# Finding the median magnitude of each token: a 31-step bisection replaced by a sum, six false-position counts and an eight-largest pass

## The reference

```python
xn = _layernorm(x)
# branch 1: a gated unit in which half of the gate's values are set to zero
s = silu(xn @ w_gate.T)                     # 2048 x 2752
idx = top_k(-abs(s), 1376)                  # the 1376 of smallest magnitude in each row
s[rows, idx] = 0
out1 = (s * (xn @ w_up.T)) @ w_down.T
# branch 2: relu(xn @ up_w)**2 @ down_w  +  (((xn @ fc1_w) @ expert_w) * route) @ fc2_w, then a layernorm
out = x + out1 + out2
```

## Time and profile before

| | us |
|---|---|
| runs: median of 3 (lowest, highest) | 2320.54 (2317.87, 2321.05) |
| the profiled execution, from its first to its last instruction | 2316.5 |
| PE busy in it | 2300.8 (99%) |
| DVE, ACT, POOL busy | 1674.1, 1112.2, 927.2 |
| DVE in the 248 counting passes of the bisection | 780.3 |
| ACT in its 248 | 655.9 |

### The profile page before, as it was taken

The page is one execution under the profiler, slowest core; times in us unless marked ns, Lnnn a source line. Parts: engine busy times, 40 slices in busy tenths (PEclk is TensorE's granted clock), DMA queues, the critical chain, the costliest instruction groups (busy, mean ns, idle before and its releaser), DMA issues.

```text
span 2316.5 us, 27959 instructions
## 1 busy us (share of the span) xinstructions
PE 2300.8 (99%) x10432; PEld 1912.1 (83%) x10432; DVE 1674.1 (72%) x1834; ACT 1112.2 (48%) x1307; POOL 927.2 (40%) x746
## 2 busy tenths in 40 slices
PE   8999999999999999999999999999999999999999
PEld 6888888888888888888888888888888888888887
DVE  4349999986366999998334599998723569999850
ACT  3247776223243688822124379780213457976110
POOL 5468988797354321333024423035004441302600
PEclk9999999999999999999999999999999999999999
DMA  7798988868899765575678875556567886555655
GB/s 285 276 402 315 334 320 305 266 238 310 300 361 331 244 227 191 195 248 178 235 232 277 283 253 193 197 193 242 203 221 254 282 268 239 192 192 195 232 191 179
DMA packets 202184, 583.61 MB, mean 252 GB/s; under 512 B 21568, under 2 KB 30784, under 8 KB 200512
## 3 DMA queue, kind: packets, MB, share of 16 engines
q1 hardware_dynamic: 202048, 581.82, 72.8%
HBM read 446.40 MB, written 135.33 MB: 251 GB/s over the span
## 4 chain that ended last, share of the span: by engine, by line
PE 82%; DVE 10%; DMA 3%; issue 2%; ACT 1%; SPq 1%; POOL 1%; DVEq 0%; ACTq 0%
PE bank L1065 26%; PE bank L1067 26%; PE bank L1066 26%; DVE junk_v L1414 3%; DVE prod L1481 2%; PE bank L1085 2%; DVE junk_v L1422 2%; DMA mixed_w<-mixes 1%; DMA split_w<-w 1%; DVE prod L1344 1%; PE bank L1076 1%; DVE acc L1385 0%; DMA w<-mixed_w 0%; SPq L631 0%; SPq L627 0%
## 5 line engine op out<-in xcount | busy, mean ns | idle before, releaser
L1414 DVE TENSOR_SCALAR_CACHE_REDUCE junk_v<-mag,cand 128x2816 bf16<-128x2816 f32 x248 | 780.3, 3146 | 8.8
L901 ACT ACTIVATE junk_s<-mag,cand 128x2816 uint8<-128x2816 f32 x248 | 655.9, 2645 | 191.6 <-DVE cand L1406 172.9
L1065 PE MATMUL bank<-w,tok 128*128 128x512 f32 (+1 forms) x808 | 309.9, 384 | 0.2 <-POOL w L845 0.2
L1067 PE MATMUL bank<-w,tok 128*128 128x512 f32 (+1 forms) x808 | 308.3, 381 | 0.0
L1066 PE MATMUL bank<-w,tok 128*128 128x512 f32 (+1 forms) x808 | 308.0, 381 | 0.0
L845 POOL TENSOR_TENSOR w<-raw,w 128x512 fp32r<-128x512 f32 (+1 forms) x196 | 267.9, 1370 | 76.5 <-ACT w L889 66.7
L1065 PE MATMUL bank<-w,prod_t 128*128 128x512 f32 x672 | 269.4, 401 | 0.0
L1067 PE MATMUL bank<-w,prod_t 128*128 128x512 f32 x672 | 262.8, 391 | 0.0
L1066 PE MATMUL bank<-w,prod_t 128*128 128x512 f32 x672 | 261.9, 390 | 0.0
L859 POOL TENSOR_TENSOR squares<-squares 128x512 f32<-128x512 f32 x64 | 67.4, 1054 | 463.9 <-ACT hidden L994 463.9
L1065 PE MATMUL bank<-tok,w 128*128 128x512 f32 x640 | 249.0, 389 | 0.0
(11 more groups left out here) (166 smaller groups left out, 4066.5 us busy)
## 6 DMA issues: line engine op xcount, KB each, us to landing
w<-split_w SPq DMA_DIRECT2D x498, 512.0 KB, 3.4
split_w<-w SPq DMA_DIRECT2D x188, 512.0 KB, 5.3
w_more<-split_w SPq DMA_DIRECT2D x66, 512.0 KB, 5.3
w<-mixed_w SPq DMA_DIRECT2D x126, 256.0 KB, 3.6
w_more<-mixed_w SPq DMA_DIRECT2D x66, 256.0 KB, 3.5
rows<-x_dram SPq DMA_DIRECT2D x32, 512.0 KB, 5.4
raw<-w_down_dram SPq DMA_DIRECT2D x44, 256.0 KB, 4.1
raw<-w_up_dram SPq DMA_DIRECT2D x40, 256.0 KB, 3.2
```

The source lines that it names most:

```text
L901: act.activation(junk_s[:, :, :], mag[:, :, t, :], ACT.Sign, scale=-1.0, bias=cand[:, t:t + 1], accum_out=cnt[:, t:t + 1]).then_inc(counte ...
L1065: pe.matmul(out, left[0], right[0], start=first, stop=False)
L1067: return pe.matmul(out, left[1], right[0], start=False, stop=last)
L1414: dve.tensor_scalar(junk_v[:, :, :], mag[:, :, t, :], cand[:, t:t + 1], float(1 - (GATED - KEPT)), ALU.is_lt, ALU.add, accum_out=cnt[:, t: ...
```

## The change

The bisection is taken out of the main path. In its place stand, for each block:

- `start_search`: three small memsets for the two ends of the bracket, then the sum of all magnitudes of a token: two passes on DVE (tiles 0, 1), two on ACT (tiles 2, 3, a Copy activation that adds up);
- `first_guess`: the upper end is twice the mean, the first try three quarters of the mean;
- six counts (`COUNTS`) at the tried value, on DVE and ACT as before (`search_step`, `count`). Between two counts `settle` now has nine small instructions instead of two: how far the count is from its aim, which end of the bracket the try replaces, and the next try by false position. The aim is 3 more than needed, give or take 3;
- `last_away` (3 small ones) and, on DVE for all four tiles, `largest_below`: a pass that writes `mag` where it is below the try and zero elsewhere (it reads `mag` as both tensor inputs), and a `max` that takes the eight largest of the result;
- `choose` picks from the eight the one that is the threshold, and compares it with the next: if these are equal for some token (a tie, or a count that did not come within 3 of its aim, in which case both are zero), the branch is entered, and in it the whole bisection of 31 steps runs, on DVE alone, before the ties are dropped as before.

The places: in blocks 1 to 3 the sum stands at e-18, the counts at e-11, e-4, e+3, e+6, e+9, e+12, the four picks at e+15, +18, +21, +24, `choose` at e+28. ACT's counts stand at DVE's numbers throughout; the special place of the third one is gone. In block 0: sum at g+5, counts at g+9, g+13, ... g+29, picks at g+33, +36, +39, +42, `choose` at g+46. `mask` moves up where its inputs allow. The buffer `below` lies over the two scratch outputs of the counting passes. Before the first block DVE sets ten more small constants. PE's, POOL's and SP's instructions stand exactly as before.

```diff
@@ Plan
-            steps_at += [last + 3 + (11 * k + 3) // 4 for k in range(BITS + 1 - len(steps_at))]
+            steps_at += [last + 3 + 3 * k for k in range(COUNTS + 2 - len(steps_at))]
         else:
             first = last + 5 if later else end[("gate", GC - 2)] + LAG + 1
-            steps_at = [first + 3 * k + (0 if later else k // 8) for k in range(BITS + 1)]
-        self.search_at = {m: k for k, m in enumerate(steps_at[:BITS])}
-        self.search_from, self.search_end = first, steps_at[BITS]
-
-        self.count_at = {m: k for m, k in self.search_at.items()}
-        if later and FAST[b] > SPILLED_PAIR:
-            self.count_at[last] = self.count_at.pop(steps_at[2])
+            steps_at = [first + 4 * k for k in range(COUNTS + 2)]
+        self.mean_at = self.search_from = first
+        self.search_at = {m: k for k, m in enumerate(steps_at[1:COUNTS + 1])}
+        self.search_end = steps_at[COUNTS + 1] + 3 * TILES + 1
+        self.pick_at = {steps_at[COUNTS + 1] + 3 * t: t for t in range(TILES)}
+        self.pick_from = steps_at[COUNTS + 1]
+        self.count_at = {first: -1, **self.search_at}
@@ ACT
                 act.wait_ge(search, b * SEARCHES + searched(k))
...
+                if k < 0:
+                    act.activation(junk_s[:, :, :], mag[:, :, t, :], ACT.Copy,
+                                   accum_out=cnt[:, t:t + 1]).then_inc(counted, 1)
@@ DVE
+            def away(b, k):
+
+                dve.wait_ge(counted, (b * (COUNTS + 1) + k + 2) * NS)
+                dve.wait_ge(search, b * SEARCHES + searched(k) + NV)
+                dve.scalar_tensor_tensor(out=tried[:, 1, :], in0=cnt[:, :], scalar=-float(2 * OFF), in1=weight[:, :],
+                                         op0=ALU.add, op1=ALU.mult).then_inc(search, 1)
+
             def settle(b, k):
...
+                away(b, k)
                 dve.wait_ge(search, at + 1)
+                dve.tensor_scalar(outside[:, 0, :], tried[:, 1, :], NEAR + 0.25, None, ALU.is_gt).then_inc(search, 1)
+                dve.tensor_scalar(outside[:, 1, :], tried[:, 1, :], -NEAR - 0.25, None, ALU.is_lt).then_inc(search, 1)
+                dve.wait_ge(search, at + 3)
+                dve.copy_predicated(ends[:, :, :, :], outside[:, :, None, :].to_broadcast([P, 2, 2, TILES]),
+                                    tried[:, None, :, :].to_broadcast([P, 2, 2, TILES])).then_inc(search, 1)
+                dve.wait_ge(search, at + 4)
+                dve.tensor_tensor(apart[:, :, :], ends[:, 1, :, :], ends[:, 0, :, :], ALU.subtract).then_inc(search, 1)
+                dve.wait_ge(search, at + 5)
+                dve.reciprocal(share[:, :], apart[:, 1, :]).then_inc(search, 1)
...
+                dve.wait_ge(search, at + 8)
+                dve.tensor_tensor(tried[:, 0, :], ends[:, 0, 0, :], share[:, :], ALU.subtract).then_inc(search, 1)
...
+            def largest_below(b, t):
+
+                at = b * SEARCHES + PICKED + 2 * t
+                dve.wait_ge(search, at)
+                dve.scalar_tensor_tensor(out=below[:, :, :], in0=mag[:, :, t, :], scalar=tried[:, 0, t:t + 1],
+                                         in1=mag[:, :, t, :], op0=ALU.is_lt, op1=ALU.mult).then_inc(search, 1)
+                dve.wait_ge(search, at + 1)
+                dve.max(largest[:, t, :], below[:, :, :].rearrange("p k n -> p (k n)")).then_inc(search, 1)
...
             def drop_ties(b):
...
+                choose(b)
                 dve.drain()
...
                 with dve.If(excess > 0):
...
+                    with dve.Fori(0, BITS):
+                        for t in range(TILES):
+                            dve.tensor_scalar(junk_v[:, :, :], mag[:, :, t, :], cand[:, t:t + 1],
+                                              float(1 - (GATED - KEPT)), ALU.is_lt, ALU.add, accum_out=cnt[:, t:t + 1])
+                            dve.drain()
```

More of the change, by code:

```diff
@@ L1394, in read_step, with start_search @@
                                                  op0=ALU.add, op1=ALU.mult).then_inc(bank_emptied[bank], 1)
+            def start_search(b):
+                at = b * SEARCHES
+                dve.wait_ge(mag_ready, (b + 1) * MAG_STEPS)
+                dve.memset(ends[:, 0, 0, :], 0.0).then_inc(search, 1)
+                dve.memset(ends[:, 0, 1, :], float(GATED - AIM)).then_inc(search, 1)
+                dve.memset(ends[:, 1, 1, :], -float(AIM)).then_inc(search, 1)
+                for i, t in enumerate(VECTOR_TILES):
+                    dve.wait_ge(search, at + 3 + i)
+                    dve.tensor_scalar(junk_v[:, :, :], mag[:, :, t, :], 1.0, None, ALU.mult, ALU.add,
+                                      accum_out=cnt[:, t:t + 1]).then_inc(search, 1)
@@ new lines, in first_guess @@
+            def first_guess(b):
+                at = b * SEARCHES + 3 + NV
+                dve.wait_ge(counted, (b * (COUNTS + 1) + 1) * NS)
+                dve.wait_ge(search, at)
+                dve.tensor_scalar(ends[:, 1, 0, :], cnt[:, :], float(PAD), 2.0 / GATED, ALU.add,
+                                  ALU.mult).then_inc(search, 1)
+                dve.tensor_scalar(tried[:, 0, :], cnt[:, :], float(PAD), 0.75 / GATED, ALU.add,
+                                  ALU.mult).then_inc(search, 1)
@@ L1519, in _ @@
             dve.memset(most[:, :], 0.0).then_inc(constants_set, 1)
-            dve.wait_ge(constants_set, 1)
+            dve.memset(weight[:, 0:NV], -1.0).then_inc(constants_set, 1)
+            dve.memset(weight[:, NV:TILES], -0.5).then_inc(constants_set, 1)
+            for i in range(8):
+                dve.memset(place[:, i:i + 1], float(i - NEAR if i < 7 else 100)).then_inc(constants_set, 1)
+            dve.wait_ge(constants_set, 11)
             normalise(0, 0, 1)
@@ L1567, in _ @@
                             settle(b, plan.search_at[m] - 1)
-                        search_bit(b, plan.search_at[m])
+                        else:
+                            first_guess(b)
+                        search_step(b, plan.search_at[m])
+                    if m == plan.pick_from:
+                        last_away(b)
+                    if m in plan.pick_at:
+                        largest_below(b, plan.pick_at[m])
                     if m == plan.search_end:
-                        settle(b, BITS - 1)
                         drop_ties(b)
```

137 lines of the change are left out of this document (97 added, 40 removed).

## The result

| | before | after |
|---|---|---|
| runs: median (lowest to highest), us | 2319.2 (2317.78 to 2321.05), 4 runs | 2340.14 (2336.38 to 2341.05), 4 runs |
| span of the profiled execution, us | 2316.5 | 2339.3 |
| ratio after / before | | 1.0088, 95% interval 1.0074 to 1.0103 |

The changed kernel is 0.9% slower, 21 us. The forecast was 2342, range 2326 to 2351. The total is right, and by luck: of its terms the block ends were put too large and block 0 too small, as the rows show, and the two errors cancel.

The account below looks back on a forecast made before the run. PE, busy 2300.8 of 2316.5 us, was taken as the bound. Block ends 15.3 plus block 0 7.3 less 0.8 gained make 21.8 us on the span; with 4.0 us from span to median, 2342 us, range 2326 to 2351.

Parts of the forecast that it names:

- What bounds the kernel: PE is busy 2300.8 of 2316.5 us; changes off PE can win only the 15.7 us idle.
- The gain between the stalls: PE's waits at each block's first transposes shrink: 0.8 us won, at most 3.
- The fast ends: Blocks 1 to 3: ACT's counts delay high parts, PE stalls 3.2 and 1.9 us a block, 15.3 in all (8 to 20).
- as it did to the two: Blocks 1 to 3: DVE reaches its nine small instructions at 783.9, when it reached the bisection's two.
- first two or three: Of DVE's nine small instructions, these end at 786.6 with POOL's work; the others take 0.2 us each.
- Block 0: Four picks hold POOL 2.9 us each, 11.6 in all; less its lead of 4.3 us, PE loses 7.3 us.
- (0 if POOL isn't held, 11 if its other work grows as well): Range given for block 0's loss of 7.3 us from the picks holding POOL.
- Only the block ends stall: Rival: POOL has more lead in block 0 or the hold is shorter; 2335 us, chance 0.17.
- half of it: Rival: `settle` is quick, 2.8 us a block at the ends, holds cost little; 2328 us, chance 0.10.
- Not slower: Rival: ACT's count doesn't wait, starting by 784.8; only the 0.8 us gain is left; 2320 us, chance 0.14.
- The eight-largest pass: Rival: it holds POOL too or takes 6 us, some 12 us more in block 0; 2354 us, chance 0.06.
- the branch: Rival: the branch with the whole bisection is entered; 2750 us, chance 0.03.

Follow-up runs that it names:

- experiment 7: Changed kernel with ACT's third counts back at e, block 0's picks at g+78 on, DVE's third counts and `settle` two granules later: 2318.74 us, 0.9999 of before.
- experiment 1: Changed kernel with ACT's third pair of counts in blocks 1 to 3 put back behind the high parts: 2332.03 us, 1.0060 of the kernel before.
- experiment 5: Changed kernel with the first `settle` of blocks 1 to 3 cut from nine small instructions to two, branch closed: 2332.45 us, 1.0059 of the kernel before.
- experiment 2: Changed kernel with block 0's four picks moved to g+78, +83, +88, +93: 2326.5 us, 1.0035 of the kernel before.
- experiment 4: Changed kernel with the first pass of block 0's picks reading `mag` once, threshold not found, branch closed: 2327.14 us, 1.0035 of the kernel before.
- experiment 3: Changed kernel with ACT's third counts back at e and block 0's picks at g+78 and on: 2320.05 us, 1.0010 of the kernel before.

## Why the forecast was right, and what in it was wrong

**What bounds the kernel: right.** PE's own work stayed the floor, and the removed 553 and 514 us on DVE and ACT bought nothing; experiment 7 shows it best, since it has the removal and none of these stalls. The gain between the stalls was 1.6 us, 0.8 forecast and 3 allowed. Of DVE's work the forecast took off some 500 us; it left out the 16 counting passes that `drop_ties` made before (L1422, 50.3 us in the profile before), which are gone too and bought as little.

**The fast ends: mechanism right, size off.** The term that was mis-sized is the time at which DVE's nine instructions are done, reckoned at 788.0; it is 786.2 in the same times, and 10.0 us took the place of 15.3. With 786.2 the forecast's own working gives 1.4 + 1.9 = 3.3 us a block, which is what was measured. Most of the 1.8 us is that both DVE and POOL are there 1.3 us sooner. DVE comes to `settle` at 782.6, and not at 783.9, "as it did to the two": the first guess before it took 1.23 + 0.16 us, where the bisection's two small instructions stood, and the sum's passes take 3.09 us, not 3.15. POOL is through with T3 at 785.1, not at 786.5. The nine themselves took 3.65 us where 783.9 to 788.0 is 4.1, two of them drawn out beside POOL, as the forecast's "first two or three". That ACT's order and the length of `settle` make this stall together is shown from both sides by experiments 1 and 5.

**Block 0: mechanism right, two parts missing.** The hold was forecast at 2.9 us, four times, and measured at 2.7 to 2.8; with 4.3 us of lead that gives 6.8, close to the 7.3 put down. What the step "(0 if POOL isn't held, 11 if its other work grows as well)" left out is ACT: its counts wait for a `settle` of 6.2 us beside a busy POOL, and POOL's own next square waits behind them for 4.25 us (2.87 in other executions). I looked at what queues behind ACT's counts only in the fast ends. That wait is free by itself (experiments 2 and 4), but once the holds have used up the lead, it counts. The second part is the granted clock, 3.0 us, a term that the forecast put at nothing without a reason: it had read that DVE's load doesn't lower it and never asked what a still PE does.

**The cancelling.** 6.6 us too little in block 0 and 5.3 too much at the ends left the total within 2 us. That is luck, and the total is no evidence for the terms; the lists of waits are.

**The rivals.** "Only the block ends stall" fell by the four stretched POOL instructions, "half of it" was right on the ends (8.4, nearer to 10.0 than my 15.3) and wrong on block 0. "Not slower" needed the count to start by 784.8, and it started at 786.2. The eight-largest pass was not dearer, 3.10 us, and the branch wasn't entered.

**What nobody had named:** the bank reads behind a `settle` of 7.6 us, 1.1 us a block, which appear only when the larger stall is removed (experiments 1 and 3).

## What to carry to other kernels

Where PE is busy for 99% of the span, count the lead of each part that PE waits for, and not the work removed elsewhere: here 550 us less on VectorE is worth nothing, and four passes that hold GpSimd for 2.8 us each cost 14. A VectorE pass with two tensor inputs belongs where GpSimd is idle or ahead by more than the pass is long, as in experiment 2; a form with one input, where the arithmetic has one, didn't hold it (experiment 4, which leaves part of the arithmetic out). And when a chain of small dependent instructions releases a queue, ask of every engine in that queue what stands behind the released instruction, and price the chain beside a busy GpSimd.

## What the hardware did that was not expected

- `scalar_tensor_tensor` with the same tensor as both inputs holds POOL as one with two tensors does: 2.70 to 2.84 us of 3.33. The eight-largest pass on 2816 float32 columns takes 3.10 us and holds nothing.
- The same nine small instructions took 3.65 us where POOL fell still behind the fourth of them, and 7.6 us where POOL worked throughout: 0.15 to 0.18 us each with POOL still, and beside it 0.15 to 0.18 for some and 1.0 to 1.2 for most. In block 0 they took 6.2 us.
- A PE that stood still for 3.97 us came back at half its clock and ran 13 matmuls in 5 us, 3.0 us lost; after 4.00 and 3.96 us in experiments 1 and 5 it lost 1.7. After 2.76 us the clock fell too; after 2.33 us it fell in one kernel and not in another. What decides was not found.
